# A keys-values attention stage regrouped: both first phases, then both second phases

## The reference

```
x = x + _L1_attn_ref(_layernorm(x), W_in, b_in, W_out, b_out, gamma, beta)

def _L1_attn_ref(X, ...):
    Xn = _layernorm(X, gamma, beta)
    Q, K, V = jnp.split(Xn @ W_in + b_in, 3, axis=-1)
    K = _rotary(K, 256); V = _rotary(V, 256)      # the first 256 columns, in pairs (even, odd)
    A = jnp.sum(_cos_sim(K) * _cos_sim(V), axis=-2)   # K/|K| * V/|V|, summed over the 2048 rows
    A = 0.5 * A + 0.5
    Y = A[:, None, :] * Q
    return Y @ W_out + b_out + X
```

## Time and profile before

| | |
|---|---|
| runs | 5289.96, 5291.74, 5298.32 us; median 5291.74 |
| the profiled execution, its own time | 5294.1 us |
| its span, first to last instruction | 5292.5 us |
| granted TensorE clock, mean | 0.950 of full speed |
| busy in the span | PE 92%, DVE 56%, ACT 42%, POOL 45% |
| the stage | 4241.3 to 4723.6 us of the span, 482.3 us |

### The profile page before, as it was taken

The page is one execution under the profiler, slowest core; times in us unless marked ns, Lnnn a source line. Parts: engine busy times, 40 slices in busy tenths (PEclk is TensorE's granted clock), DMA queues, the critical chain, the costliest instruction groups (busy, mean ns, idle before and its releaser), DMA issues. The chain is left out here.

```text
span 5292.5 us, 93390 instructions
## 1 busy us (share of the span) xinstructions
...
## 2 busy tenths in 40 slices
...
GB/s 211 82 89 95 103 80 260 129 75 76 76 73 72 76 74 74 74 74 76 76 64 175 177 82 103 100 85 113 125 95 95 59 73 51 39 101 55 48 53 35
DMA packets 247902, 485.88 MB, mean 92 GB/s; under 512 B 31058, under 2 KB 85330, under 8 KB 247124
## 3 DMA queue, kind: packets, MB, share of 16 engines
...
...
## 5 line engine op out<-in xcount | busy, mean ns | idle before, releaser
L1324 DVE TENSOR_REDUCE attend_mx<-attend_am_ps 128x1 f32<-128x1024 f32 x1024 | 1214.8, 1208 | 361.8 <-PE attend_am_ps L1204 361.8
L1311 POOL TENSOR_TENSOR attend_pairs<-attend_pt 128x1024 f32<-128x1024 f32 x512 | 1261.1, 2464 | 306.9 <-ACT attend_pt L1295 306.3
L1295 ACT ACTIVATE attend_pt<-attend_sc_ps 128x512 f32<-128x512 f32 x2048 | 1113.3, 595 | 647.2 <-PE attend_sc_ps L1193 600.9
L1193 PE MATMUL attend_sc_ps<-attend_qst,attention_kst 98*128 98x512 f32 x2048 | 801.2, 432 | 7.1 <-ACT attend_pt L1295 7.1
L1204 PE MATMUL attend_am_ps<-attention_kst,attend_qst 96*128 96x512 f32 x2048 | 666.7, 408 | 12.1 <-DMA attend_qst<-q_parts 8.7
L1193 PEld LDWEIGHTS attend_sc_ps<-attend_qst,attention_kst 98*128 98x128 f32 x2048 | 344.8, 188 | 372.4 <-ACT attend_pt L1295 263.2
L1222 PE MATMUL attend_pv_ps<-attend_pt,attention_v 128*32 128x256 f32 x8192 | 548.6, 385 | 0.4 <-ACT attend_pt L1295 0.4
L715 DVE TENSOR_TENSOR expert_ac<-expert_gu_ps,expert_gl 128x512 f32<-128x512 f32 x144 | 99.6, 692 | 669.6 <-ACT expert_gl L679 669.5
L1204 PEld LDWEIGHTS attend_am_ps<-attention_kst,attend_qst 96*128 96x128 f32 x2048 | 391.5, 193 | 117.6 <-DVE attend_mx L1324 45.8
L1724 DVE SCALAR_TENSOR_TENSOR ffn_hf<-ffn_gu_ps,ffn_us,ffn_sg 128x256 f32<-128x256 f32 x352 | 170.7, 485 | 396.5 <-ACT ffn_sg L1671 396.5
L1671 ACT ACTIVATE ffn_sg<-ffn_gu_ps,ffn_gs 128x256 f32<-128x256 f32 x352 | 167.4, 476 | 508.2 <-PE ffn_gu_ps L1608 508.1
...
## 6 DMA issues: line engine op xcount, KB each, us to landing
attend_pairs<-attend_pairs POOLq DMA_DIRECT2D x192, 512.0 KB
...
ys<-expert_ob SPq DMA_DIRECT2D x144, 256.0 KB
attend_qst<-q_parts SPq DMA_DIRECT2D x192, 128.0 KB
yn<-route_yb SPq DMA_DIRECT2D x64, 256.0 KB
ffn_xb<-x SPq DMA_DIRECT2D x64, 256.0 KB
ffn_rb<-x SPq DMA_DIRECT2D x64, 256.0 KB, 3.0
...
```

The source lines that it names most:

```text
L1193: pe.matmul(sc[:, g, :], kst[0:KROWS + 2, b * S + kt * P:b * S + (kt + 1) * P], qst[0:KROWS + 2, k, hh:hh + 4, :], start=True, stop=True). ...
L1295: act.activation(pt[:, u % RING, g * 4 * P:(g + 1) * 4 * P], sc[:, g, :], ACT.Exp, scale=HD ** -0.5).then_inc(p_rdy, 1)
L1311: pool.tensor_tensor(pairs[:, j, :], pt[:, 2 * p % RING, :], pt[:, (2 * p + 1) % RING, :], ALU.add).then_inc(pair_rdy, 1)
L1324: dve.tensor_reduce(mx[:, u // 2, u % 2:u % 2 + 1], am[:, u % 2, :], AX.X, ALU.max).then_inc(mx_rdy, 1)
```

## The change

The stage is rewritten. Both first phases run as one sequence of 32 tiles, then both second phases; the transposes of all 32 tiles are kept (`yT`). Loops over pairs of tiles become straight code.

- The second layer norm is folded into the first: a second norm of a normalised row only rescales it. VectorE takes one set of statistics (`stats`), ScalarE two roots (`roots`), VectorE a reciprocal and two small products (`scales`), and ScalarE normalises (`normalise`). `yb`, `xy` and their instructions go; in the second phase x is loaded again (`reload`) and ScalarE computes x plus its norm (`whole`).
- The columns of the rotated half are ordered even, then odd. Since only the products of rotated keys with rotated values are needed, GpSimd multiplies keys with values and turns the products by the double angle: eight operations for each tile, two over 256 elements and six over 128.
- VectorE adds the weighted products up over a batch (`gather`, 512 elements), and TensorE sums over the rows once for each batch.
- M is made piece by piece beside other tiles: for batch 0 in steps 18 to 22 of the first phase, for batch 1 in steps 2 to 6 of the second. The part of the bias row that comes from beta is made on VectorE (`query_bias`, step 4). The batch's row sums are taken in step 17 (`shares`).
- The keys-values weights are loaded in four pieces that GpSimd issues; ScalarE makes the high part. `keysvalues(0)` now comes before the bias matmuls.
- SyncE's queue: in step t it waits for `y2` of tile t, loads x of tile t+2, waits for `turn_rdy` of tile t (GpSimd's seventh operation on tile t) and loads the angles of tile t+2. VectorE takes the statistics of tile t+3 in step t, behind the keys-values copy of tile t (`evacuate(t)`) and ahead of that of tile t+1.

```
...
+            def load(t):
+                sp.dma_start(xb[:, t % 2, :], x[bass.ds(t * P, P), :]).then_inc(x_in[t % 2], 16)
+            def load_angles(t):
+                sp.dma_start(cs[:, t % 2, :], angles[bass.ds(t % NB * P, P), :]).then_inc(cs_in[t % 2], 16)
+            load(0)
+            load(1)
+            for to, src in ((gam, gamma), (bet, beta), (bq, b_q)):
+                sp.dma_start(to[:], src).then_inc(sm["small_in"], 16)
+            sp.dma_start(bkv[:].rearrange("p v d -> p (v d)"), b_kv.partition_broadcast(P)).then_inc(sm["bkv_in"], 16)
+            load_angles(0)
+            load_angles(1)
+            for to, src in ((bet_row, beta_row.partition_broadcast(P)), (wq[:], w_qT), (wo[:], w_out)):
+                sp.dma_start(to, src).then_inc(sm["wo_in"], 16)
+            for t in range(NT):
+                if t + 2 < NT:
+                    sp.wait_ge(sm["y2_rdy"], t + 1)
+                    load(t + 2)
+                if t == 0:
+                    sp.wait_ge(sm["bk_rdy"], 1)
+                    sp.dma_start(bo[:, 0, :], b_out.partition_broadcast(P)).then_inc(sm["bo_in"], 16)
+                if t + 2 < NT:
+                    sp.wait_ge(sm["turn_rdy"], t + 1)
+                    load_angles(t + 2)
+            def reload(t):
+                sp.dma_start(xb[:, t % NX, :], x[bass.ds(t * P, P), :]).then_inc(xs_in[t % NX], 16)
+            sp.wait_ge(sm["y2_rdy"], NT)
+            reload(0)
+            reload(1)
+            sp.wait_ge(sm["tr_rdy"], NT)
+            reload(2)
+            reload(3)
+            sp.wait_ge(sm["nrm_rdy"], NT)
+            sp.dma_start(bo[:, 1, :], b_out.partition_broadcast(P)).then_inc(sm["bo_in"], 16)
+            for t in range(NT):
+                sp.wait_ge(sm["ob_rdy"], t + 1)
+                sp.dma_start(x_out[bass.ds(t * P, P), :], ob[:, t % 2, :]).then_inc(o_st[t % 2], 16)
+                if t + NX < NT:
+                    reload(t + NX)
...
+            turn(0)
+            keysvalues(0)
+            bias()
+            turn(1)
+            for t in range(NT):
+                if t + 2 < NT:
+                    turn(t + 2)
+                if t == SUMS_AT + 1:
+                    sums(0)
+                if t + 1 < NT:
+                    keysvalues(t + 1)
+                if PARTS_AT <= t < PARTS_AT + DC:
+                    mixed(0, t - PARTS_AT)
+                if t == PARTS_AT + DC:
+                    mixed_bias(0)
...
+            for t in range(NT):
+                out(t)
+                if t == 0:
+                    sums(1)
+                if LATE_PARTS <= t < LATE_PARTS + DC:
+                    mixed(1, t - LATE_PARTS)
+                if t == LATE_PARTS + DC:
+                    mixed_bias(1)
...
+            for c in range(DC):
+                pool.dma_start(raw[:, 2 * c:2 * c + 2, :], w_kv[:, 2 * c:2 * c + 2, :]).then_inc(w_in[c], 16)
+            pool.memset(eps2[:], LN_EPS * LN_EPS).then_inc(sm["eps_rdy"], 1)
+            for t in range(NT):
+                k = t % 2
+                keys, values = kv[:, k, 0, :], kv[:, k, 1, :]
+                pool.wait_ge(sm["kv_kept"], t + 1)
+                pool.wait_ge(cs_in[k], 16 * (t // 2 + 1))
+                pool.tensor_tensor(pr[:, 0:2, :], keys[:, 0:ROT].rearrange("p (h d) -> p h d", h=2), values[:, 0:ROT].rearrange("p (h d) -> p h d", h=2), ALU.mult).then_inc(sm["pr_rdy"], 1)
+                pool.tensor_tensor(pr[:, 2, :], keys[:, 0:HR], values[:, HR:ROT], ALU.mult).then_inc(sm["pr_rdy"], 1)
+                pool.tensor_tensor(pr[:, 3, :], keys[:, HR:ROT], values[:, 0:HR], ALU.mult).then_inc(sm["pr_rdy"], 1)
+                pool.wait_ge(sm["pr_rdy"], 3 * t + 1)
+                pool.tensor_tensor(dx[:, 0, :], pr[:, 0, :], pr[:, 1, :], ALU.subtract).then_inc(sm["dx_rdy"], 1)
+                if t:
+                    pool.wait_ge(sm["acc_rdy"], t)
+                pool.tensor_tensor(prod[:, 0:HR], pr[:, 0, :], pr[:, 1, :], ALU.add).then_inc(sm["rot_rdy"], 1)
+                pool.wait_ge(sm["pr_rdy"], 3 * t + 3)
+                pool.tensor_tensor(dx[:, 1, :], pr[:, 2, :], pr[:, 3, :], ALU.add).then_inc(sm["dx_rdy"], 1)
+                pool.wait_ge(sm["dx_rdy"], 2 * t + 2)
+                pool.tensor_tensor(dx[:], dx[:], cs[:, k, :].rearrange("p (n d) -> p n d", n=2), ALU.mult).then_inc(sm["turn_rdy"], 1)
+                pool.wait_ge(sm["turn_rdy"], t + 1)
+                pool.tensor_tensor(prod[:, HR:ROT], dx[:, 0, :], dx[:, 1, :], ALU.subtract).then_inc(sm["rot_rdy"], 1)
...
+            def roots(t):
+                k = t % 2
                 act.wait_ge(sm["mv_rdy"], t + 1)
+                if t >= 2:
+                    act.wait_ge(sm["rs_rdy"], t - 1)
+                act.activation(sd[:, k, 0:1], mv[:, k, 1:2], ACT.Sqrt, bias=const["eps"][:]).then_inc(sm["sd_rdy"], 1)
+                act.activation(sd[:, k, 1:2], mv[:, k, 1:2], ACT.Sqrt, bias=eps2[:], scale=1.0 + LN_EPS).then_inc(sm["sd_rdy"], 1)
...
+            def normalise(t):
+                k = t % 2
+                act.wait_ge(sm["shift_rdy"], t + 1)
+                if t >= 2:
+                    act.wait_ge(sm["tr_rdy"], t - 1)
+                act.activation(y2[:, k, :], xb[:, k, :], ACT.Identity, bias=shift_x[:, t, 1:2], scale=rs[:, k, 1:2]).then_inc(sm["y2_rdy"], 1)
...
+            for t in range(NT):
+                if t + 2 < NT:
+                    high(t + 2)
+                    keep(t + 2)
+                if t + 3 < NT:
+                    roots(t + 3)
+                squares(t)
+                if t + 3 < NT:
+                    normalise(t + 3)
+                if PARTS_AT <= t < PARTS_AT + DC:
+                    mixed(0, t - PARTS_AT)
+            def whole(t):
+                act.wait_ge(xs_in[t % NX], 16 * (t // NX + 1))
+                act.wait_ge(sm["scale_rdy"], t + 1)
+                act.activation(xb[:, t % NX, :], xb[:, t % NX, :], ACT.Identity, bias=shift_x[:, t, 0:1], scale=scale_x[:, t:t + 1]).then_inc(sm["xy_rdy"], 1)
...
+            def stats(t):
+                k = t % 2
+                dve.wait_ge(x_in[k], 16 * (t // 2 + 1))
+                dve.bn_stats(bn[:, k, :], xb[:, k, :]).then_inc(sm["bn_rdy"], 1)
+                dve.wait_ge(sm["bn_rdy"], t + 1)
+                if t >= 2:
+                    dve.wait_ge(sm["shift_rdy"], t - 1)
                 dve.tensor_copy(pause[:], const["eps"][:])
+                dve.bn_aggr(mv[:, k, :], bn[:, k, :]).then_inc(sm["mv_rdy"], 1)
...
+            def scales(t):
+                k = t % 2
+                dve.wait_ge(sm["sd_rdy"], 2 * (t + 1))
+                if t >= 2:
+                    dve.wait_ge(sm["y2_rdy"], t - 1)
+                dve.reciprocal(rs[:, k, :], sd[:, k, :]).then_inc(sm["rs_rdy"], 1)
                 dve.wait_ge(sm["rs_rdy"], t + 1)
+                dve.tensor_scalar(shift_x[:, t, :], rs[:, k, :], mv[:, k, 0:1], -1.0, ALU.mult, ALU.mult).then_inc(sm["shift_rdy"], 1)
+                dve.tensor_scalar(scale_x[:, t:t + 1], rs[:, k, 0:1], 1.0, None, ALU.add).then_inc(sm["scale_rdy"], 1)
...
+            def low(t):
                 dve.wait_ge(sm["thi_rdy"], t + 1)
+                dve.wait_ge(sm["yT_rdy"], t + 1)
+                dve.tensor_tensor(t_lo[:, t % 2, :], tr[:, t % 2, :], t_hi[:, t % 2, :].bitcast(F32), ALU.subtract).then_inc(sm["tlo_rdy"], 1)
...
+            def evacuate(t):
+                k = t % 2
+                dve.wait_ge(sm["kv_rdy"], t + 1)
+                if t == 0:
+                    dve.wait_ge(sm["bk_kept"], 1)
+                if t >= 2:
+                    dve.wait_ge(sm["rot_rdy"], 2 * (t - 1))
+                    dve.wait_ge(sm["nrm_rdy"], t - 1)
+                dve.tensor_tensor(kv[:, k], kv_ps[:, k], bkv[:], ALU.add).then_inc(sm["kv_kept"], 1)
+            def plain(t):
+                k = t % 2
+                dve.wait_ge(sm["kv_kept"], t + 1)
+                if t:
+                    dve.wait_ge(sm["acc_rdy"], t)
+                dve.tensor_tensor(prod[:, ROT:D], kv[:, k, 0, ROT:D], kv[:, k, 1, ROT:D], ALU.mult).then_inc(sm["pass_rdy"], 1)
+            def gather(t):
+                k, b = t % 2, t // NB
+                dve.wait_ge(sm["nrm_rdy"], t + 1)
+                dve.reciprocal(rn[:], nrm[:, k, :]).then_inc(sm["rn_rdy"], 1)
+                dve.wait_ge(sm["rn_rdy"], t + 1)
+                dve.tensor_tensor(rr[:], rn[:, 0:1], rn[:, 1:2], ALU.mult).then_inc(sm["rr_rdy"], 1)
+                dve.wait_ge(sm["rr_rdy"], t + 1)
+                dve.wait_ge(sm["pass_rdy"], t + 1)
+                dve.wait_ge(sm["rot_rdy"], 2 * t + 2)
+                if t % NB == 0:
+                    dve.tensor_scalar(acc[:, b, :], prod[:], rr[:], None, ALU.mult).then_inc(sm["acc_rdy"], 1)
+                else:
+                    dve.scalar_tensor_tensor(acc[:, b, :], prod[:], rr[:], acc[:, b, :], ALU.mult, ALU.add).then_inc(sm["acc_rdy"], 1)
...
+            for t in range(NT):
+                evacuate(t)
+                if t:
```

(56 more changed lines are left out.)

498 lines of the change are left out of this document (192 added, 306 removed).

## The result

| | before | after |
|---|---|---|
| median of 8 runs each | 5295.89 us | 5313.11 us |
| lowest to highest | 5289.96 to 5303.32 | 5307.07 to 5317.97 |
| ratio, 95% interval | | 1.0033, 1.0023 to 1.0042 |
| span of the profiled execution | 5292.5 | 5307.6 |
| the stage, from its first load of x to the next stage's | 485.6 | 500.3 |

The changed kernel is 17 us slower at the median. The profiled executions differ by 15.1, the stage by 14.7, so nothing else moved. From here on, the stage is measured as in the last row, because it begins up to 10 us earlier or later from one execution to the next. One run of the kernel before, at 8021.8 us and a granted clock of 0.55, is left out of every ratio.

The account below looks back on a forecast made before the run. A closed one-tile ring through SyncE's queue was taken as the bound: 29.5 + 322 + 20 + 14 + 8 + 87 + 17 + 5 + 2 = 504.5 us against 482.3, so 5291.7 + 22 = 5314 us, range 5266 to 5345.

Parts of the forecast that it names:

- last two copies: End of the first phase: the two copies without statistics take 7 us each, 14 together.
- last copy to first output matmul: Handover to the outputs: GpSimd's eight operations, `acc` and `low_again`, 8 us that no tile hides.
- outputs, second M, last additions: Second phase: 32 outputs 87 us, second M 17, cold start and waits for the shares 5, last additions 2.
- The ring: First phase: x queued behind angles that wait for GpSimd closes a one-tile ring, 11.1 us a turn (9.5 to 12.0).
- the hold-up: Inside each turn: VectorE's `rr`, `acc` and plain product behind the copy delay GpSimd by 1.15 us (0 to 1.4).
- the sign: VectorE idle 2 to 4 us each turn ahead of the statistics, ended by the DMA of x, some 90 us in all.
- The start: Stage start to first keys-values copy, which waits for the bias row: 29.5 us (27 to 35), 37.4 before.
- The longer steps: VectorE turns with `query_bias` 5.7, `shares(0)` 3 and five pieces of M 11: together 20 us (12 to 28).
- Cheap ring: Rival: no hold-up by VectorE and short GpSimd price, 9.5 to 10 us a tile, 5273 us; chance 0.17.
- No ring: Rival: x lands in time or the queue is not held, 7.5 us a tile, 5210 us; chance 0.13.
- Cold TensorE: Rival: idle TensorE drops to 1.2 GHz, its matmuls make the copy late by 2 us, 5357 us; chance 0.10.
- The Trainium skill's two rules: VectorE and GpSimd contend for shared SBUF interfaces; issuing x's DMA earlier gains 3.4 us, a narrower x tile nothing.

Follow-up runs that it names:

- apart: The changed kernel with VectorE's work behind the copy moved into its wait for x, and `prod` in two buffers: 5299.2 us, 1.0012 of before.
- best: x_ahead with ScalarE normalising between the two squares, tile 1's transposes ahead of the bias matmuls, and output low parts ahead of the last gather: 5190.8 us.
- x_ahead: The changed kernel with SyncE's load of x of tile t+3 issued before the wait for GpSimd's seventh operation on tile t: 5207.5 us, 0.9832 of before.

## Why the prediction was right, step by step

The forecast was 5314 by a ring of 11.1 us a turn. The median is 5313.1 and the turn 10.60. Part of the closeness is luck. In the stage, 22 us more were forecast and 14.7 measured (497 against 482.3): the turns were put 14 us too long and the start 7.6 too short. And the forecast was added to a median of three runs, 5291.7, where that of eight is 5295.9: 4.2 us too low a base hides most of the rest. The change of the medians is 17.2.

| term | forecast | measured |
|---|---|---|
| start to first copy | 29.5 (27 to 35) | 37.1 |
| ordinary turn | 11.1 | 10.6 |
| 29 turns without what is longer in them | 322 | 308 |
| longer steps | 20 | 21 |
| last two copies | 14 | 13.2 |
| last copy to first output matmul | 8 | 7.6 |
| outputs, second M, last additions | 111 | 109.7 |
| sum | 504.5 | 497 |

- **The ring.** Right in place and cause, and near in each link. GpSimd's seven operations and the hold-up were put at 4.5 and took 4.24; SyncE and the flight at 3.42 and took 3.15; statistics and scales at 2.0 and took 1.92. Inside GpSimd's term the two halves were off: alone the operations take 3.63 (3.35 forecast), and the hold-up is 0.61 (1.15 forecast), as apart shows. A 128-element operation takes 0.46, between the two lines of the forecast (0.35 and 0.48). VectorE's wait ahead of the statistics is 4.2 us a turn and 124.4 in all, where 2 to 4 and some 90 were named as the sign: its own work in a turn is shorter than I had it. SyncE's x follows the angles after 0.37, not 0.5.
- **The start.** Here the step failed: 37.1 lies outside its bounds. It took the bias row as the last thing before the first copy. But on TensorE the transposes of tile 1 stand behind the bias matmuls, and on VectorE `low(1)`, statistics and scales of tile 2 stand ahead of the addition of the bias row:

```profile
4266.90 7.03 PE L1875 MATMUL keyvalue_kv_ps<-keyvalue_raw,keyvalue_bo 128*128 128x512 f32 x16
4273.77 0.60 PE L1852 MATMUL keyvalue_tr_ps<-all_ident,keyvalue_xb 128*128 128x128 f32 x4
```

```profile
4275.60 0.69 DVE L2089 TENSOR_TENSOR keyvalue_t_lo<-keyvalue_tr_ps,keyvalue_t_hi 128x512 fp32r<-128x512 f32 x1 [13.45 <-ACT keyvalue_yT L1993]
...
4278.12 1.22 DVE L2181 TENSOR_TENSOR keyvalue_bkv<-keyvalue_kv_ps,keyvalue_bkv 128x1024 f32<-128x1024 f32 x1
```

  The bias ends at 4273.9 and is added at 4278.1, 4.2 us later. In best, with the transposes moved, it is added as soon as it is there (4280.28, behind matmuls that end at 4280.2). Link by link, forecast and measured:
  - The parts of the weights are ready 14.5 and 19.8 us into the stage. The four low parts alone take VectorE 4.86 us (4257.29 to 4262.15), where 2.5 was put for all parts.
  - The keys-values matmuls that are left then take 2.5 and 4.8. They begin at 4258.71, and at a granted clock of 0.50 (4258.7 to 4264.0) they did not keep up with the parts, as I had assumed.
  - The bias matmuls take 11.3 and 7.0, at a granted clock of 1.00 (4266.9 to 4273.8).
  - The order on VectorE costs 0 and 4.2, and the addition 1.2 and 1.3.

  That is 29.5 and 37.1.
- **The longer steps.** The query bias cost 5.7, as forecast, the shares 1.9 (3 forecast), the five pieces of M 13.5 (11 forecast).
- **Cheap ring.** Its two conditions were no hold-up and the short price. The hold-up was half of the forecast's and the price the long one; 10.6 lies between the two cases (9.5 to 10, and 11.1).
- **No ring.** 5210 forecast under its condition, 5207.5 measured when x_ahead makes the condition true. Here too the low base helps: a tile takes 7.07 us, not 7.5.
- **Cold TensorE.** It was given its own case, as if the clock stayed either high or low. It was low for about a third of each tile's matmuls. They began 2.3 us into the turn (4403.69), as forecast, but ended 9.65 into it and not by 8: hidden by 0.95 us in after, and late by 0.3 to 0.7 in some turns of apart.
- **The Trainium skill's two rules.** GpSimd and VectorE do hold each other up where VectorE has two SBUF inputs. `rr` (4402.75) ends at 4403.38, with GpSimd's first operation (4403.37), and GpSimd's third operation takes 0.91 beside `acc` (0.91) and 0.46 in apart, where `acc` takes 0.75. `low`, with one input in PSUM, takes 0.69 beside GpSimd. By the rule (GPSIMD Engine Reference, key points) that is what should happen, and the trace agrees. The rule to issue a DMA early and wait late (DMA: Bandwidth & Descriptors, rules for kernel authors) agrees too: with x issued earlier, VectorE's wait for it falls from 124.4 us to 5.9. The gain is 3.5 us a turn (10.60 to 7.07), near the 3.4 that the prediction gave to SyncE and the flight. That is a coincidence: once the ring is open, the gain ends where the next bound stands, the 7.07 us of the other engines. The 2 us of fixed cost stand on that page for DMAs that GpSimd issues; here SyncE issues, and 256 KB land 2.7 us after the issue. That a narrower x tile gains nothing does not follow from the rule, and none was tried.
